# A pre-norm attention and gated feed-forward layer on one core: batch 1's rope and batch 0's memory products moved, GpSimd's order changed, one more up chunk in the last score phase

## What is computed

```python
q, k, v = hn @ Wq.T, hn @ Wk.T, hn @ Wv.T          # hn = layernorm(x)
q, k = rope(q), rope(k)
k_feat, q_feat = elu(k) + 1, elu(q) + 1             # per head
memory = einsum('bhsd,bhse->bhde', k_feat, v)
mem_out = (q_feat @ memory) / (q_feat @ k_feat.sum(s))
attn = softmax(q @ k.T * scale) @ v
x = x + (sigmoid(gate) * mem_out + (1 - sigmoid(gate)) * attn) @ Wo.T
up = silu(ln(x) @ W1.T) * (ln(x) @ W3.T)
x = x + fwht(up) @ W2.T                             # Walsh-Hadamard over the 1024 columns
```

## Time and profile before

| | |
|---|---|
| median of 3 runs | 217.6 us (216.65 to 218.44) |
| the profiled execution's own time | 218.47 us |
| its span, first to last instruction | 216.7 us |
| PE busy in the span | 193.2 us, 89% |
| DVE / ACT / POOL busy | 148.2 / 99.2 / 92.0 us |
| mean granted TensorE clock | 0.976 of full speed |

### The profile page before, as it was taken

The page is one execution under the profiler, slowest core; times in us unless marked ns, Lnnn a source line. Parts: engine busy times, 40 slices in busy tenths (PEclk is TensorE's granted clock), DMA queues, the critical chain, the costliest instruction groups (busy, mean ns, idle before and its releaser), DMA issues.

```text
span 216.7 us, 4078 instructions
## 1 busy us (share of the span) xinstructions
PE 193.2 (89%) x1476; PEld 164.2 (76%) x1476; DVE 148.2 (68%) x329; ACT 99.2 (46%) x199; POOL 92.0 (42%) x84
## 2 busy tenths in 40 slices
PE   7898898499995998999979999996689988979993
PEld 3396797347794997878968998785589966869993
DVE  6499898963899963569898636299796345754442
ACT  3356715287722344884024368840215677231330
POOL 7719999990003895342039521320112231030332
PEclk9999999957999999999999999999999999997999
DMA  6998620003430000053100000533000100001001
GB/s 179 356 371 186 188 70 0 9 0 80 116 105 0 2 9 0 0 153 99 53 0 0 3 8 0 148 91 110 0 3 6 48 3 2 0 3 48 0 3 48
DMA packets 12639, 13.54 MB, mean 62 GB/s; under 512 B 1388, under 2 KB 11852, under 8 KB 12620
## 3 DMA queue, kind: packets, MB, share of 16 engines
q1 hardware_dynamic: 11148, 11.96, 18.6%
q10 hardware_dynamic: 1472, 1.32, 2.2%
HBM read 5.71 MB, written 1.05 MB: 31 GB/s over the span
## 4 chain that ended last, share of the span: by engine, by line
issue 38%; PE 27%; POOL 23%; DVE 7%; ACT 2%; POOLq 1%; DVEq 0%; ACTq 0%
PE exp_bank L1087 5%; POOL hid_lo L577 5%; PE score_bank L1144 4%; POOL w_lo L603 4%; PE score_bank L1087 3%; POOL prod L569 3%; PE exp_bank L1091 3%; PE down_bank L1109 2%; POOL narrow_raw L584 2%; POOL w_lo L596 2%; DVE prod L709 2%; POOL w_lo L617 2%; DVE rowmax_pad L698 2%; POOL part_lo L565 2%; PE score_bank L1091 2%
## 5 line engine op out<-in xcount | busy, mean ns | idle before, releaser
L577 POOL TENSOR_TENSOR hid_lo<-wide_raw,hid_hi 128x256 fp32r<-128x256 f32 x32 | 23.9, 747 | 71.4 <-ACT hid_hi L419 71.4
L698 DVE TENSOR_REDUCE rowmax_pad<-score_bank 128x2 f32<-128x512 f32 x64 | 42.8, 681 | 4.3 <-PE score_bank L978 4.2
L384 ACT ACTIVATE prob<-exp_bank 128x512 f32<-128x512 f32 x64 | 37.0, 601 | 17.2 <-PE exp_bank L996 16.7
L978 PE MATMUL score_bank<-k_stack,q_stack 128*128 128x256 f32 x128 | 27.3, 303 | 8.6 <-DVE rowmax_pad L698 8.5
L996 PE MATMUL exp_bank<-q_stack,k_stack 128*128 128x256 f32 x128 | 27.6, 318 | 4.1 <-DMA q_stack<-nmT_lo 2.3
L996 PEld LDWEIGHTS exp_bank<-q_stack,k_stack 128*128 128x128 f32 x128 | 19.9, 203 | 11.7 <-ACT prob L384 6.7
L978 PEld LDWEIGHTS score_bank<-k_stack,q_stack 128*128 128x128 f32 x128 | 19.3, 189 | 12.2 <-DVE rowmax_pad L698 8.3
L551 POOL TENSOR_TENSOR rstd<-var_eps,mhalf 128x2 f32<-128x2 f32 x8 | 5.6, 704 | 37.5 <-DVE var_eps L671 37.5
L806 DVE SCALAR_TENSOR_TENSOR wide_raw<-wide_raw,score_bank 128x256 f32<-128x256 f32 x16 | 6.7, 417 | 20.0 <-ACT wide_raw L413 20.0
L413 ACT ACTIVATE wide_raw<-exp_bank 128x256 f32<-128x256 f32 x16 | 6.1, 384 | 29.1 <-PE exp_bank L1091 27.1
L1087 PE MATMUL exp_bank<-h2T_hi,w_hi 128*128 128x256 f32 x64 | 17.8, 300 | 0.7 <-ACT h2T_hi L404 0.7
(11 more groups left out here) (142 smaller groups left out, 483.2 us busy)
## 6 DMA issues: line engine op xcount, KB each, us to landing
q_stack<-part_hi SPq DMA_DIRECT2D x16, 128.0 KB
k_stack<-part_hi SPq DMA_DIRECT2D x14, 128.0 KB
xs<-in_x SPq DMA_DIRECT2D x4, 256.0 KB, 3.2
prob<-in_w2T SPq DMA_DIRECT2D x1, 1024.0 KB, 9.4
wide_raw<-in_w1T SPq DMA_DIRECT2D x1, 1024.0 KB, 11.4
wide_raw<-in_w3T SPq DMA_DIRECT2D x1, 1024.0 KB, 12.8
q_stack<-part_lo SPq DMA_DIRECT2D x8, 128.0 KB
k_stack<-part_lo SPq DMA_DIRECT2D x7, 128.0 KB
```

The source lines that it names most:

```text
L384: act.activation(prob[:, h % 8], exp_bank[h % 2][:], ACT.Exp, scale=SCALE).then_inc(prob_s, 1)
L577: pool.tensor_tensor(hid_lo[:, n % 3, :], ffn_work[n % 3], hid_hi[:, n % 3, :].bitcast(F32), ALU.subtract).then_inc(hid_lo_s, 1)
L698: dve.tensor_reduce(rowmax[:, h, :], score_bank[h % 2][:], AX.X, ALU.max).then_inc(rowmax_s, 1)
L978: mm = pe.matmul(bank[:, tt, :], q_stack[:, h, tt * P:tt * P + P], k_stack[:, h, :], start=True, stop=True)
```

## The change

Round 0: the four rope products of batch 1 go from between the row maxima to behind them (the first ahead of `low_max`, three behind it, and the layer-norm statistics of batch 2 behind those); `memory(0)` goes from behind scores 13 to behind scores 15, its masking from behind maximum 14 to behind maximum 15. POOL does both butterflies first in round 0, then rope sum 0, `ln_power`, rope sum 1, the negative part and the low parts; the low part of W2 goes from round 1 to the end of round 0. ACT does `split_w2` between `split_max` and `evac_lin`, and the two `split_parts` of batch 1 ahead of the first two exponentials. PE issues two `keep_clock` matmuls behind `read_memory`. Round 3: the up halves of batch 2 begin at h = 8 in place of 10, so that chunks 0 to 3 are in the score phase, chunk 4 takes chunk 3's place at the hinge, and the exp phase loses the up halves at h = 0 and 1; two gates move up on DVE, and chunk 3 of batch 2 uses an exp bank.

```diff
@@ chunk_bank
-            return (exp_bank if n % FC in (7, 0, 1, 2) else score_bank)[n % 2]
+            early = (7, 0, 1, 2, 3) if n // FC == NB - 2 else (7, 0, 1, 2)
+            return (exp_bank if n % FC in early else score_bank)[n % 2]
@@ scalar
-                if has(r + 1):
+                if r >= 1 and has(r + 1):
                     split_parts(r + 1, 0)
...
                 if has(r):
                     split_max(r)
+                if r == 0:
+                    split_w2()
...
                 for h in range(NH):
+                    if r == 0 and h < DC:
+                        split_parts(1, h)
                     if has(r):
                         exp_head(r, h)
...
                     evac_att(r, 2)
-                if r == 0:
-                    split_w2()
@@ gpsimd
-                if has(r + 1):
+                if r == 0:
+                    butterfly(pool, 0)
+                    butterfly(pool, 1)
+                    rope_sums(1, 0)
+                    ln_power(LN[(1, 2)])
+                    rope_sums(1, 1)
+                    negative_part(1)
+                    low_parts(1)
+                elif has(r + 1):
                     rope_sums(r + 1, 0)
-                if has(r + 1):
                     rope_sums(r + 1, 1)
                 hid_low(chunk(r - 2, 7))
-                if has(r + 1):
+                if r >= 1 and has(r + 1):
                     low_parts(r + 1)
-                if r == 1:
-                    pool.wait_ge(w2_hi_s, 1)
-                    pool.tensor_tensor(w2_lo[:], w2_b, w2_hi[:].bitcast(F32), ALU.subtract).then_inc(w2_lo_s, 1)
-                if r == 0:
-                    butterfly(pool, 0)
-                    ln_power(LN[(1, 2)])
-                if has(r + 1):
                     negative_part(r + 1)
-                if r == 0:
-                    butterfly(pool, 1)
...
+                if r == 0:
+                    pool.wait_ge(w2_hi_s, 1)
+                    pool.tensor_tensor(w2_lo[:], w2_b, w2_hi[:].bitcast(F32), ALU.subtract).then_inc(w2_lo_s, 1)
@@ vector
-                    if h == 12 and r == 0:
+                    if h == 13 and r == 0:
                         memory_strips(0)
-                    if 3 <= h < 7 and has(r + 1):
+                    if 3 <= h < 7 and r > 0 and has(r + 1):
                         rope_product(r + 1, h - 3)
...
-                    if h == 12:
+                    if h == (12 if r < NB - 1 else 10):
                         ffn_gate(chunk(r - 1, 0))
+                    if h == 12 and r == NB - 1:
+                        ffn_gate(chunk(r - 1, 1))
                 if r == 0:
-                    ln_statistics(LN[(1, 2)])
+                    rope_product(1, 0)
                 if has(r):
                     low_max(r)
                 if r == 0:
+                    for k in range(1, 4):
+                        rope_product(1, k)
+                    ln_statistics(LN[(1, 2)])
                     gate_weights()
-                ffn_gate(chunk(r - 1, 1))
+                if r < NB - 1:
+                    ffn_gate(chunk(r - 1, 1))
@@ tensor
-                    if h == 11 and r == 0:
+                    if h == 13 and r == 0:
                         memory(0)
...
-                    for i in UP_AT[h]:
+                    for i in UP_AT[h] if r < NB - 1 else (h - 8,) if h >= 8 else ():
                         ffn_up(chunk(r - 1, i // 2), i % 2)
...
                     read_memory(r, 1)
+                if r == 0:
+                    keep_clock(2)
                 for m in range(2):
-                    ffn_up(chunk(r - 1, 3), m)
+                    ffn_up(chunk(r - 1, 3 if r < NB - 1 else 4), m)
...
-                    if h in UP_IN_EXP:
+                    if h in UP_IN_EXP and (r < NB - 1 or h > 1):
```

## The result

The changed kernel takes 216.28 us in the median of 14 runs, the kernel before 218.39 us in its 14; the ratio is 0.989, with a 95% interval from 0.985 to 0.993. That is 2.1 us less; 1.95 us less had been forecast. The profiled execution of the changed kernel took 215.03 us, its span is 213.3 us.

A forecast was written before the change was run, and what follows sets the result against it. PE, busy 89% of the span, was taken as the bound, with a DVE chain behind round 0's waits; -1.4 - 0.9 + 0.35 = -1.95 us, from the median 217.6 to 215.6, range 213.5 to 217.9.

The forecast's parts named there:

- the three terms: Round 0 passes on 1.4 us, round 1 gains 0.9 us, round 3 loses 0.35 us.
- Part 1: Score phase of round 0: `transpose_max` 2.2 us earlier, PE could begin shifted scores 3.1 us earlier, two `keep_clock` matmuls (0.94) free.
- Part 2: ACT in round 0: first exponential 1.1 us earlier; its phase ends about 4.3 us earlier if PE's clock stays up.
- Part 3: Round 0: POOL's low part of W2 holds DVE's combine; first maximum of batch 1 1.15 us earlier, 1.4 us passed on.
- Part 4: Round 1: with the low part of W2 gone from POOL, PE's wait for the first `hid_lo` goes, 0.9 us.
- Part 5: Round 3: moved up halves make `transpose_max` about 1.1 us later, the exp phase gives some back; 0.35 us slower.
- The full gain of round 0: Rival: low part of W2 doesn't hold DVE, clock stays up or falls shortly; round 0 passes on 3.0 us, 214.1; 30%.
- the second: Rival: PE's gap in round 0's shifted scores lets the clock fall, round 0 passes on nothing, 217.05; 15%.
- `features`: Rival: in round 0 `features` stands behind POOL's low part of W2 until 54.6; +1.3 us overall, 218.9; 11%.

The follow-up runs named there:

- held kernel before: Kernel before plus unread matmuls: two behind `read_memory` in round 0, others in the score phases of rounds 1 and 3 and the tail; 215.34 us, ratio 0.988.
- W2 late: Changed kernel, but POOL begins the low part of W2 only behind the last piece of batch 0's combine; 218.03 us, ratio 1.000.
- the halves: Changed kernel with round 3 as before, low part of W2 in two halves (second behind the combine) and a few unread matmuls; 214.14 us, ratio 0.983.
- round 0 only: Changed kernel with round 3 as in the kernel before; 214.4 us, ratio 0.986.

## Why the prediction was right, and where it was not

**The number.** 1.95 us less were forecast and 2.1 measured. Between the profiled executions the three terms came out at -1.17, -1.11 and +0.64 us, -1.64 together. The rest of the median's 2.1 lies, I think, in how often the clock falls elsewhere, for one in the tail, where a fall costs 1.5 us: no execution of before in the list kept it, three of 14 after did. That remainder I infer from the list above, I did not isolate it. So the nearness of 1.95 and 2.1 is in part luck: each term was off by 0.2 to 0.3 us, two in one direction and one in the other, and what made up for it stood in no term.

**Part 1** holds: `transpose_max` 2.0 us earlier (forecast 2.2), the shifted scores 2.5 (3.1). One term was mis-sized. I read four records of 1.88 us as four matmuls; they are two, so `keep_clock(2)` takes 1.88 us and not 0.94, runs past the landing of the maxima, and costs 0.27 us there, as the run without it shows. ACT hides that. In the kernel before with four such matmuls the records say the same: eight of them, 3.60 us.

**Part 2** holds in size: the first exponential is 1.0 us earlier (forecast 1.1), behind `split_w2` at 38.08, which waited for the butterflies. What follows was mis-sized: I had ACT's exponentials end 4.3 us earlier if the clock stays up, and counted from the common mark they end 2.5 us earlier (31.83 and 34.37), with waits for PE of 0.35 and 0.70 us still between them. The lock of part 3 hides that too.

**Part 3** holds in its wait, and that was the point that decided the number: the long operation of POOL holds DVE's product until it ends, for 1.70 us in place of 0.18 with the clock up and for 0.58 with it down, and the operation moved away lets the maximum come 1.4 us earlier. The first maximum of batch 1 came 1.04 us earlier (forecast 1.15), the rstd 1.17 (1.4). The Trainium skill ("SBUF — State Buffer", section "SBUF: two separate sides") says that the lock is held for the whole instruction; the 4.55 and 4.58 us operations here agree with it, by the ends at 53.65 with 53.61 and 62.96 with 62.94.

But the cause that I gave for round 0's gain was wrong in one step: I compared with the old order as it ran, its clock down for 7 us, and credited the difference to the moved work. The held kernel before shows that the old order at full clock has the same rstd (41.46) and an earlier first maximum (32.24). So moving rope, memory and butterflies is worth nothing at the rstd of round 1 by itself, and by the estimate above the changed order, with its lock, is even behind there. What it changes is that PE's gap no longer has to cost anything: either the clock stays up, or POOL's operation ends later than ACT's work anyway.

**Part 4** holds: no wait for `hid_lo`, 1.1 us (forecast 0.9); it comes back with the operation. A condition was missing: where the clock falls in the score phase of round 1, the old order doesn't wait there either (4.58 and 4.67 us), and nothing is gained.

**Part 5** holds in sign and mechanism: 1.38 us later at `transpose_max` and 0.69 given back, +0.64 instead of +0.35.

**The rivals.** The full gain of round 0 did not come, since the lock held. Nor do its 3.0 us come without the lock: in W2 late and in the halves the rstd is 1.5 us earlier than before (41.17 and 41.14 against 42.65), with 0.8 to 1.05 us lost to an unread matmul or to the 128x2 operation ahead of it; so I estimate some 2.4. Of the second, the fall of the clock came in some executions (round 0 only, at 44 to 47), but not its price: the rstd is at 41.49 there too. `features` did not get behind the long operation: it began at 46.33, POOL's at 49.06.

## What to carry to other kernels

Before crediting an order of work with a gain, compare the granted clock in the stretch of both traces; here a few unread matmuls, with nothing moved, bought the same 2 us. The new order of rounds 0 and 1, the operation in halves and such matmuls, with round 3 left as it was, bought 3.5; what the halves alone are worth no run separates. Put such a matmul only where PE waits: one that stood where DVE waited for PE cost 0.8 us there. A long GpSimd operation costs VectorE whatever is left of it when a two-input product wants to start, so put it where VectorE works out of PSUM (beside the 4.58 us operation of W2 late a row maximum took its usual 0.69 us), or cut it at the point where the product is due. Count matmuls by the code and not by the records.

## What the runs showed of the hardware that I had not expected

- The clock falls not only behind the one long gap. It fell in the score phase of round 1 (68 to 75 in the kernel before with four unread matmuls), where the longest single wait of PE was 1.43 us, and in that of round 3; with one unread matmul behind h = 1 and one behind h = 4 of both phases the mean clock was 0.997 or more in the six runs of the halves and in the six of the held kernel before.
- A fall isn't always paid: round 0 of the changed kernel took the same time with it and without (33.16 and 33.15), since DVE waited for POOL.
- A 128x512 fp32 matmul leaves two records. One shows 1.02 us, two 1.88 and four 3.60, so each further one holds PE 0.86 us.
- A VectorE tensor_scalar from SBUF to SBUF beside a running GpSimd operation does not always stand until that ends, so part 3's reading of the rows was too wide. Normalising two 128x256 blocks took 1.45 us at 42.46 in the kernel before (0.73 in other rounds) and ended at 43.91, beside POOL's negative part of 42.41 to 45.18; in the changed kernel it took 2.47 us, partly beside POOL's rope sum. How much of that is waiting, and why the 128x2 operation stood, no run here separates.
